# The down-projection's first half in a score bank, and the exponential's table loaded early, in an early-fusion transformer on one core

## The reference

```python
h = silu(patches(x) @ tW1 + b1) @ tW2 + b2; h = concatenate([h, txt], 1)      # (64, 228, 256)
def attn(x):                                         # called with layernorm(h)
    xn = rms_norm(x) * ln1_w
    q, k, v = normalize(xn @ Wq), normalize(xn @ Wk), xn @ Wv       # 16 heads of 16
    p = softmax(mask((q @ k.T + bias) * scale))
    y = (p @ v) @ Wo + x
    z = relu(rms_norm(y) * ln2_w @ W1) @ W2          # W2: the down-projection, 1024 -> 256
    return z + y
h = h + attn(layernorm(h))
h = h + experts(layernorm(h))                        # each of 8 experts takes its best quarter of all rows
```

## Time and profile before

| | us |
|---|---|
| median of 3 runs | 4234.71 (4230.84 to 4241.97) |
| the profiled execution: its time | 4228.73 |
| its span, first to last instruction | 4226.9 |
| TensorE busy with matmuls | 3665.6 (87%) |
| DVE busy | 2624.3 (62%) |
| ScalarE busy | 2081.8 (49%) |
| GpSimd busy | 1748.1 (41%) |
| mean granted TensorE clock | 0.951 |

### The profile page before, as it was taken

How to read it: one execution, slowest core, us unless ns; L and a number is a source line. 1 busy time by engine, 2 the same in 40 slices (tenths; PEclk the granted TensorE clock), 3 DMA queues, 4 the chain that set the end, 5 groups by cost and what they waited for, 6 DMA issues and landing times. The chain is left out here.

```text
span 4226.9 us, 83054 instructions
## 1 busy us (share of the span) xinstructions
PE 3665.6 (87%) x28702; PEld 2376.2 (56%) x28702; DVE 2624.3 (62%) x5223; ACT 2081.8 (49%) x3393; POOL 1748.1 (41%) x1395
## 2 busy tenths in 40 slices
PE   2788888888889889889899898259999999999998
PEld 1466666666656656656666666135555555555554
DVE  3666766766666666666666665675555555555554
ACT  1544444444454454444444443326656555655655
POOL 1223333233233233233233231026666666666666
PEclk9899999999999999999999998569999999999999
DMA  7322312312322222222222210713333323323223
GB/s 137 43 37 43 50 37 42 50 37 42 50 40 43 47 41 46 41 45 46 38 47 48 34 30 10 211 36 46 65 64 46 65 45 66 63 44 66 46 46 46
DMA packets 297490, 219.83 MB, mean 52 GB/s; under 512 B 107846, under 2 KB 284680, under 8 KB 297208
## 3 DMA queue, kind: packets, MB, share of 16 engines
q1 hardware_dynamic: 188562, 155.40, 19.2%
q0 software_dynamic: 107264, 62.29, 9.5%
q10 hardware_dynamic: 1496, 0.01, 0.0%
HBM read 115.76 MB, written 62.74 MB: 42 GB/s over the span
## 5 line engine op out<-in xcount | busy, mean ns | idle before, releaser
L1690 DVE SCALAR_TENSOR_TENSOR hTs<-hTe,scales,hTs 128x456 f16<-128x456 f32 x514 | 322.7, 686 | 446.8 <-ACT hTs L1194 446.8
L1496 DVE TENSOR_TENSOR pr<-pr,bias_t 114x684 f32<-114x684 f32 x512 | 476.0, 955 | 175.6 <-ACT pr L1063 175.4
L1865 POOL DMA_INDIRECT out_dram<-contrib,idx_cur x256 | 537.5, 2100 | 109.4 <-issue 78.9
L554 PE MATMUL G<-w2m,hT 128*114 128x256 f16 x3072 | 424.8, 299 | 87.0 <-DVE stage L1468 87.0
L1063 ACT ACTIVATE pr<-SC 114x684 f32<-114x684 f32 x512 | 378.3, 745 | 240.7 <-PE SC L477 240.0
L937 PE MATMUL SC<-xgT,ws 128*128 128x456 f16 x2316 | 469.3, 357 | 0.0
L554 PEld LDWEIGHTS G<-w2m,hT 128*114 128x114 f16 x3072 | 385.3, 146 | 95.7 <-DVE stage L1468 94.9
L1858 POOL DMA_INDIRECT xg<-xn_rows,idx_cur x264 | 377.8, 1431 | 117.3 <-issue 61.2
L396 PE MATMUL G<-img,w1t 128*128 128x392 f32 x768 | 343.3, 538 | 74.5 <-DMA img<-turned 57.1
L937 PEld LDWEIGHTS SC<-xgT,ws 128*128 128x128 f16 x2316 | 227.4, 98 | 221.2 <-issue 3.7
L537 PE MATMUL SC<-yT,w1m 128*128 128x456 f16 x1536 | 318.0, 357 | 18.5 <-ACT yT L1095 11.2
(11 more groups left out here) (269 smaller groups left out, 6957.9 us busy)
## 6 DMA issues: line engine op xcount, KB each, us to landing
raw<-in_x_dram SPq DMA_DIRECT2D x192, 196.0 KB, 6.2
img<-turned SPq DMA_DIRECT2D x384, 98.0 KB, 2.8
we<-in_L_ffn_W_dram SPq DMA_DIRECT2D x34, 1024.0 KB, 7.7
out_dram<-stage SPq DMA_DIRECT2D x32, 456.0 KB
xn_rows<-stage SPq DMA_DIRECT2D x32, 456.0 KB
xg<-xn_rows,idx_cur POOLq DMA_INDIRECT x264, 3.7
out_dram<-contrib,idx_cur POOLq DMA_INDIRECT x256, 5.5
bias_by_distance<-pr SPq DMA_DIRECT2D x1, 2429.6 KB, 30.1
```

The lines of the kernel that those rows point to most:

```text
L554: last = pe.matmul(part.g("w2", b)[0:T, at:at + D], hT[:, hp, m, t * T:(t + 1) * T], w2m[:, wp, m, :], start=m == 0 and i == 0, stop=m == ...
L1496: dve.tensor_tensor(pr[g % 4][:, :, :], pr[g % 4][:, :, :], bias_t[:, 2 * pair:2 * pair + 2, :], ALU.mult).then_inc(probs_done, 1)
L1690: dve.scalar_tensor_tensor(hTs[:, 1, m, :], hTe[:, m, :], scale_at(scales, 2, e), hTs[:, 0, m, :], ALU.mult, ALU.subtract).then_inc(h_spli ...
L1865: pool.indirect_dma_start(out=out_rows, out_offset=bass.IndirectOffsetOnAxis(ap=idx_cur[k4][:, t:t + 1], axis=0), in_=contrib[k][:, t, :], ...
```

## The change

The first half of the down-projection goes to the score bank `SC[1][:, 1, :]`, with two semaphores of its own, and so no longer waits for or holds up the second half in `G[0]`. All 16 pieces run ahead of the first transposes. Before piece 0 TensorE waits for all eight blocks of `hT`. The first half is taken out behind `qk_norm` instead of within it; the scores of group 1, which use that bank, wait for it. The second half is taken out behind group 1 instead of 5, and the statistics follow behind group 3 instead of 6. ScalarE does an exponential of one element behind the high parts of queries and keys, so that the table's load comes there.

```diff
-            [("tok2", 0)] + ... + BANKED["qkv"][0] + [("w2", 0), ("w2", 1)],
+            [("tok2", 0)] + ... + BANKED["qkv"][0] + [("w2", 1)],
...
             if g == 1 and not first:
-                pe.wait_ge(router_copied, j)
+                pe.wait_ge(first_half_taken, j)
...
+        def w2_bank(part, b):
+            return SC[1][:, 1, :] if b == 0 else part.g("w2", 1)
...
-                if n % 8 == 0:
-                    part.wait_free(pe, "w2", b)
+                if n == 0:
+                    pe.wait_ge(hid_low_done, MC * j + MC)
+                if n == 8:
+                    part.wait_free(pe, "w2", 1)
...
-                if n % 8 == 7:
-                    pe_block(part, ("w2", b), last)
+                if n == 7:
+                    last.then_inc(first_half_made, 1)
+                if n == 15:
+                    pe_block(part, ("w2", 1), last)
...
-        for n, slot in enumerate((0, 2, 4, 5)):
-            SLOTS[slot].append(("w2", range(12 + n, 13 + n)))
...
-            for n in range(0, 12, 2):
+            for n in range(0, 16, 2):
                 w2(n)
             pe_qkT(part, j, 0)
...
                 high_parts(i, range(NT))
+                act.activation(warm[:, 1:2], warm[:, 0:1], ACT.Exp).then_inc(exp_loaded, 1)
                 exps(part, i)
...
                                       ALU.mult).then_inc(qk_scaled, 1)
-                if part.kind != "first":
-                    mlp_out(part, j - 1, 0)
                 for t in range(NT):
                     dve.wait_ge(qk_high, NT * j + (t + 1))
...
-                    if not first and g == 5:
+                    if not first and g == 1:
                         mlp_out(part, j - 1, 1)
-                    if not first and g == 6:
+                    if not first and g == 3:
                         mlp_stats(part)
...
                 qk_norm(part, i)
+                mlp_out(part, i - 1, 0)
                 masked_probs(part, i)
```

More of the change, by code:

```diff
@@ L197, in early_fusion_kernel @@
         w_sums = s1("w_sums", [128, 5])
+        warm = s1("warm", [1, 2])
         w_norms = s1("w_norms", [128, 6])
@@ L287, in early_fusion_kernel @@
         ones_ready, xs_high, y2_high = sem("ones_ready"), sem("xs_high"), sem("y2_high")
+        first_half_made, first_half_taken, exp_loaded = sem("first_half_made"), sem("first_half_taken"), sem("exp_loaded")
         hid_made, hid_high, hid_low_done = sem("hid_made"), sem("hid_high"), sem("hid_low_done")
@@ L322, in early_fusion_kernel @@
         body = (
-            [("tok2", 0)] + BANKED["after"][0] + BANKED["front"][0] + BANKED["qkv"][0] + [("w2", 0), ("w2", 1)],
+            [("tok2", 0)] + BANKED["after"][0] + BANKED["front"][0] + BANKED["qkv"][0] + [("w2", 1)],
             [("tok2", 1)] + BANKED["after"][1] + BANKED["front"][1] + BANKED["qkv"][1] + BANKED["qkT"],
@@ L330, in early_fusion_kernel @@
             "final": (body[0] + BANKED["turn"], body[1]),
-            "last": (BANKED["after"][0] + [("w2", 0), ("w2", 1)], BANKED["after"][1]),
+            "last": (BANKED["after"][0] + [("w2", 1)], BANKED["after"][1]),
         }
@@ L553, in pe_w2 @@
                     for i, (wp, hp) in enumerate(PARTS):
-                        last = pe.matmul(part.g("w2", b)[0:T, at:at + D], hT[:, hp, m, t * T:(t + 1) * T], w2m[:, wp, m, :],
+                        last = pe.matmul(w2_bank(part, b)[0:T, at:at + D], hT[:, hp, m, t * T:(t + 1) * T], w2m[:, wp, m, :],
                                          start=m == 0 and i == 0, stop=m == MC - 1 and i == len(PARTS) - 1)
-                if n % 8 == 7:
-                    pe_block(part, ("w2", b), last)
+                if n == 7:
+                    last.then_inc(first_half_made, 1)
+                if n == 15:
+                    pe_block(part, ("w2", 1), last)
         SLOTS = {n: [] for n in range(2 * NG)}
-        for n, slot in enumerate((0, 2, 4, 5)):
-            SLOTS[slot].append(("w2", range(12 + n, 13 + n)))
         for slot, work in ((17, ("yq", 0)), (20, ("yq", 1))):
@@ L579, in pe_slot @@
                     pe_turn(part, j, work[1])
-                elif work[0] == "w2" and part.kind != "first":
-                    pe_w2(part, j - 1, work[1])
         def pe_attention(part, j):
@@ L1292, in _ @@
             last.then_inc(qkv_folded, 1)
+            dve.memset(warm[:, :], 0.0)
             dve.memset(sum_ones[:, :], 1.0).then_inc(ones_ready, 1)
@@ L1464, in mlp_out @@
                 dve.wait_ge(hy_done, 2 * (j + 1))
-                part.wait_filled(dve, "w2", b)
+                if b == 0:
+                    dve.wait_ge(first_half_made, j + 1)
+                else:
+                    part.wait_filled(dve, "w2", 1)
                 for half in range(2):
                     t = 2 * b + half
-                    last = dve.scalar_tensor_tensor(hy[:, t, :], part.g("w2", b)[0:T, half * D:(half + 1) * D],
+                    last = dve.scalar_tensor_tensor(hy[:, t, :], w2_bank(part, b)[0:T, half * D:(half + 1) * D],
                                                     r2[:, t:t + 1], hy[:, t, :], ALU.mult, ALU.add)
-                last.then_inc(evacuated[part.bank("w2", b)], 1)
+                last.then_inc(first_half_taken if b == 0 else evacuated[part.bank("w2", 1)], 1)
             def mlp_stats(part):
```

## The result

The changed kernel takes 4324.85 us, median of 4 runs (4321.68 to 4329.25), beside 4232.77 us (4227.16 to 4241.97) for the kernel before on the same chip: ratio 1.0212, 95% interval 1.0195 to 1.0229. The forecast was 4299 us, 1.5% slower, with a range of 4190 to 4335. The sign came true and the copy strikes as foreseen, but a second cause, the clock in the attention front, is much larger than the prediction had it. The time fell 26 us short.

The account below looks back on a forecast made before the run. TensorE's waits for DVE's L1468 (87.0 us in all) were the target. Terms -1.75 - 0.7 + 2.4 + 1.8 + 0.6 = +2.35 us in each of 29 pairs, -3.7 for the last two, gave 4299 us, range 4190 to 4335.

Parts of the forecast that it names:

- Part 1: Down-projection: all 96 matmuls run in one piece, so the first transpose comes 1.75 us earlier per pair.
- Part 2: Exponential's table: its load moves into ScalarE's idle time, bringing group 7's scores 1.01 us earlier against the first transpose.
- Part 3: Attention front: pieces leaving give -0.5 us, early statistics cost +0.8; with the load's -1.01, group 7's scores stand at -0.7.
- Part 4: Earlier statistics bring GpSimd's copy onto DVE's multiplication of group 10 or 11, delaying `yn` and TensorE: +2.4 us per pair.
- Part 5: Granted clock: +1.8 us behind TensorE's new idle time, +0.6 (bounds 0 and 1.5) in the attention front, per pair.
- (a): Rival: the copy strikes group 12 or later, where DVE has slack; 4177 us, or about 4205 with more low clock; 22%.
- (b): Rival: the copy strikes but the clock holds behind it, without the 1.8 us; 4247 us; 13%.
- (c): Rival: the table load still stands behind the wait for scores, +1.0 us per pair; 4330 us; 4%.

Follow-up runs that it names:

- e9: Kernel before with the table loaded behind the high parts, and unread matmuls in the stall, ahead of the transposes and in groups 3 to 7; 4231.49 us.
- e4: Kernel before with only the one-element exponential added behind the high parts, so the table loads early; 4229.10 us, ratio 0.9995.
- e8: Changed kernel with late second half and statistics, six unread matmuls per group 0 to 7, three ahead of transposes, but no early table load; 4207.96 us.
- e5: Changed kernel plus unread matmuls: three ahead of the first transposes and six ahead of the scores of each group 0 to 7; 4313.12 us.
- e6: Changed kernel with six unread matmuls per group 0 to 7, three ahead of transposes, and second half and statistics back behind groups 5 and 6; 4191.38 us.
- e1: Changed kernel with GpSimd's copy behind the normalisation cut to an eighth of its columns, for timing alone; 4271.54 us, ratio 1.0098.
- e2: Changed kernel with the second half taken out behind group 5 and the statistics behind group 6, as before; 4309.11 us, ratio 1.0177.
- e11: Changed kernel with late second half and statistics, two unread matmuls per group 0 to 7 and three ahead of the transposes; 4143.36 us, ratio 0.9796.
- e12: Changed kernel with late second half and statistics, one unread matmul per group 0 to 7 and three ahead of the transposes; 4169.50 us, ratio 0.9856.

## Why the prediction was right, and where it was off

**Part 1, the down-projection: right in kind, -1.41 for -1.75.** The matmuls ran in one piece, but TensorE waited 0.45 us for the last copy of `qkp`, which DVE ended 42.97 us after the pair's start (1605.62 + 0.21 - 1562.86) where the prediction had 42.57. DVE is the condition that comes last, which the prediction had 0.2 us the other way. It also counted the half clock's 1.79 us with the stall's 2.78, and e9 bears that out in kind: filling the stall at full clock gives 1.03 us without any bank moved.

**Part 2, the table: right in kind, -0.7 for -1.0.** The load lies where it was said to, and group 7 comes at 14.10 with it alone (e4), in the pairs without a second stretch. 0.41 us per pair are seen where fillers pace the front (e8).

**Part 3, the front's order: too dark, as far as the runs show.** The statistics behind group 3 were to cost 0.8 us. In fronts that something else paces nothing of it is seen: 15.19 with them and 15.20 without under six fillers (e5, e6), 16.65 and 16.64 with much half clock (e1, e2). In pair 19 of the kernel after, where the clock is back by then, a little is: DVE's last copy of keys comes without idle time behind group 4's multiplication, which had to follow the statistics, and group 7's scores wait 1.06 us for it where group 5's wait 0.80, so some 0.3. DVE's copy, then TensorE's scores of group 7:

```profile
1702.10 0.63 DVE L1449 COPY qkT<-G 128x912 f16<-128x912 f16 x1
...
1702.86 0.31 PE L477 MATMUL SC<-qkT 64*114 64x228 f16 x2 [1.06 <-DVE qkT L1449]
```

At full clock, with the statistics late, the front without pieces takes 13.3 to 13.5 us (e11, e12), fillers included. The prediction's own terms without the 0.8 give 13.3 as well (14.80 - 1.01 - 0.5); with it they gave 14.1.

**Part 4, the copy: right, but it doesn't decide the sign.** The chain from the statistics to the copy, a multiplication and `yn` is there; the copy strikes group 10 in 14 pairs, group 9 in 12 and group 8 in 3, where the prediction had 10 or 11. But the prediction also had every kernel in which the copy misses faster than before. e1 is slower than before although its copy holds up nothing, and pair 30, which has no copy and was to gain 1.85 us, lost 3.87 (82.32 - 78.45): the front's clock alone makes the change a loss. In e5, where the front's clock doesn't blur it, the copy starts 22.3 us behind the first transpose (prediction 21.7), group 10 at 23.0 (21.9), and it costs 1.95 us (2.4). In the kernel after it starts at 22.9, since the slow front brings the statistics later (their end 14.6 us behind the first transpose, not 12.6), while GpSimd needs 8.3 us from there instead of 9.1. That the four normalisations hold up a multiplication as well is barely seen: those that start beside one take 1.07 us at most after and 0.93 before, for 0.86.

**Part 5, the clock: right behind the strike, mis-sized in the front.** Behind the strike +1.8 was charged, and e5 has 2.45; in the kernel after only the pairs like 19 have it. In the front the term was +0.6, with 1.5 as its upper bound. It comes to 16.44 - 13.3 = 3.1 us, if the front at full clock is taken from e12, whose statistics are late; with the whole 0.8 us that the prediction had for early ones it would still be 2.3. This is the term that was far off. The prediction took its size from pair 15 of the kernel before, one stretch of 3.4 us of low clock in a front that still had its pieces. Without them the stretch that begins in the front is 6.8 us long in the pairs like 19, 17.1 in those like 18, and 20.5 in pair 30. What was mild in 5 of 28 pairs was a bound from below.

Sum, per pair, with the front at full clock taken at 13.3 us as above, an estimate: -1.41 to the first transpose; in the front -1.58 by what the change does (13.3 against 14.88) and +3.14 by the clock; +3.23 behind it: +3.38, as the trace has. Against the prediction's terms that is +0.34, -0.88, +2.54 and -0.97 (3.23 for 2.4 + 1.8), together +1.03 on its +2.35. Two errors to the dark side hid most of the one in the front's clock, and the range held the time partly for that reason: that much of the hit is luck.

**The rivals.** (a), the copy misses, was put at 4177 to 4205. e1 and e2 show that taking the copy away or moving it doesn't get there (4272, 4309); e6, with both causes taken away, is at 4191. (b), the clock holds behind the strike: true of one pair of 28 in e5, and in the kernel after of the pairs like 18, which pay in the front instead. (c), the load isn't hidden: false.

What stays open: why the clock in e12 falls in 6 pairs of 28 that do the same as the others up to the fall, why it falls in 24 of 28 in e4, and what exactly brings it back. The runs show that matmuls between the waits of the front keep it. How much TensorE stands in all doesn't settle it: 3.3 us of the front at full clock in e4, where it mostly falls (14.10 - 10.79), and as much in e11, where it never does (pair 18, 13.45 - 10.13). How e11 would do without the three fillers ahead of the transposes, or with the early statistics, wasn't tried.

## What to carry to other kernels

Work that fills an engine's waits may be what keeps its clock: before taking matmuls out from between waits, read the granted clock of that stretch in every kind of pair the trace has, and price the stretch at half clock throughout, not at one dip. When a change does what it should and the time doesn't follow, put matmuls that nobody reads into the waits: it is a cheap test, and here two per group (and three ahead of the front) turned the 1.8% loss of e2 into a gain of 2.0%. A handoff that is moved earlier takes along what waits for it on a third engine; look for what that instruction then meets, here a multiplication of 0.87 us that became 2.91.

## What the runs showed of the hardware

The clock fell to half in a front whose single waits are about 1.1 us at most (1.08 in the timeline of pair 18), with TensorE busy 1.55 of the first 3.00 us, and stayed there while it was busy 10.53 of 14.00. It held at 10.15 of 13.50 in e11. Since half clock makes the engine busier for the same work, a busy share read at half clock says little about whether the clock could be kept. Nor does one read at full clock say all: e12's pairs 20 and 21 do the same up to the fall. The Trainium skill (TensorE: Matmul & The Clock Gate, A second HAM failure mode: psum-queue depth-cycling) tells of another kernel in which short idle times between groups of matmuls make the clock swing; these runs agree, and add that filling part of the idle times stops it.

Work for nothing can pay many times over: e11 has 19 fillers of 0.11 us per pair more than e2, 2.1 us of matmuls, and takes 166 us less, some 5.3 us in each of 31 pairs.

GpSimd's copy and DVE's multiplication of two SBUF tensors hold each other up, whichever is first. The multiplication that starts within the copy ends 0.7 us behind it. The copy takes 2.80 to 2.88 us where no multiplication is under way at its start, as in pair 19, and 3.37 to 3.39 where one is, in the 29 such copies of the kernel before; in pair 18 of the kernel after it is 3.26.
